# Two transformer layers on one core: a first pass fed from on-chip transposes, and a last layernorm's output written by Pool

## Chip, cores and metric

One NeuronCore of one Trainium2 chip. The metric is the device time of one launch in microseconds. Engines: PE (TensorE), DVE (VectorE), ACT (ScalarE), POOL (GpSimd, below also Pool) and SP (SyncE, which here only issues transfers).

## The reference, cut to what matters

x has 4 batches of 1024 tokens with 128 channels, 16 heads of 8 channels. Four residual blocks follow each other, each ended by a layernorm:

```python
x = _layernorm(x + L0_attn(x))   # q, k scaled to norm 1 per token; softmax over all 1024 keys; projection
x = _layernorm(x + L0_ffn(x))    # int8 quantised matmul 128x128
x = _layernorm(x + L1_attn(x))   # layernorm of q, k per head, rotary table, causal softmax; projection
x = _layernorm(x + L1_ffn(x))    # silu(gate) * up, hidden 384, then down
```

In layer 0's attention q and k are divided by their norm over the 128 channels of a token, and the scores by 8**0.5 and by the head's temperature.

## The kernel before

**Work.** The tokens are eight chunks of 512. Attention runs in 64 passes: a layer, a batch, a half of its queries (512) and a group of four heads. Passes are taken in pairs, and a pair is cut into steps; there are 400 steps. A step is two exps on ACT (`probs<-ps`, line 717, 128x1024 each) with the scores before them (`scores`, line 874, into one of three slots of two PSUM banks) and the sums behind them (`sums`, line 896, four heads side by side into the bank `ACC`). In layer 1 the steps on the causal diagonal are masked by Pool (`mask`, line 627) between the exp and the sums.

**Heads stacked by products.** A head's 8 channels of q and k are written as a high and a low part (tf32-like `fp32r`), and the four products of the parts are stacked as rows: in `q_st` and `k_st` each group of 32 rows (a head) holds 8 channels times 4 products. The stacks of a pass come from `parts_scratch` in DRAM: `send_parts` (line 449) writes the parts, `load_rows` (line 465) reads the rows. Pass 0 and pass 1 are special: their rows are copied from the tile `prep_part` by small transfers (`first_rows`, line 424, 64 KB each).

**Side work.** All that isn't attention is cut into units: projections, norms, transposes, the two feed-forward blocks. PE's units go through one PSUM bank (`SIDE`); DVE reads it and frees it (`side_filled`, `side_read`). Each lane of units (`p` for layer 0's q, k, v; `m` for the middle; `l` for the last block; `t` for what ends a pair) is in a fixed order. The table `ORDER` has one word for each of the 400 slots and one behind: it says how many units of which lane are run there, and with `<` or `|` whether the sums come behind the side units or between the two scores. PE, DVE, Pool and SP all build their programs from this table.

**The head**, before the first exp: DVE's `memset` feeds warm-up matmuls (`keep_warm`, line 930), PE makes q, k and v of chunks 0 and 1 in eight banks (line 938), ACT squares q and k of each token tile with a running sum (line 689), DVE takes the reciprocal root of 8 sums in nine small steps (`rows_norm`, lines 1103 and 259 to 271) and scales k and q (line 1117). PE transposes them (line 752), ACT and DVE cut them into parts (lines 700 and 1332 to 1336), and SP and ACT copy the rows of pass 0 with four transfers each. PE waits for `parts_ready` and `rows_in[0]`. The second half of the keys of pass 0 comes by four more transfers from SP (line 515), that of pass 1 through DRAM. `WARM` counts warm-up matmuls.

**Lines that the change touches besides:** the output of the last layernorm of chunks 0 to 6 (units `ln_out_y`, lane `l`; chunk 6 in lane `m`) is four `tensor_scalar` of 128x128 by DVE (line 1075, `yo<-last_y`), and SP stores `yo`. Chunk 7 is done by `end()`. The matmul of layer 0's feed-forward (`ffn`, line 838) is four bf16 matmuls of 128x128 for a chunk; other PE units are cut by `quarters` (line 763) into 32 output columns of the array at a time. Pool's program is a list sorted by slot:

```python
todo = [(s + 1, 0, "mask", s) for s in range(NS) if STEPS[s][3]]
...
todo += [(FIRST[p - 1], 3, "bias", p) for p in range(GB - 1, NP, GB)]
todo.sort(key=lambda x: x[:2])
```

Of the kernel before, what the change touches and what calls it, by code (L numbers as in the profile page):

```python
# [166 lines left out]
lp m m |t <mm mmp <mm <m p m <p <mpp <m <mp <m m <mtt <mm |m |tm
m p <m mp ll <mll m - ll < <l < |tl l l l - |l < l
- l < l < <llll l l |t | |tt mm m <t m mm <mm | |tmm |
|ttl l <lm <m |mm <mml mml m < m m mmm - l t mlm lm ml m |l  # L170
ml ml < <m l l l <ll <l <lm tt < tm <m <m |mm |m |mm |m mm
- |mmlmm | |tmm | |m m < m < m <l <m m m <m |tm | |tmtlm -
<m <ll mm ml < m < ll - <l | <l tl - | |l l l - <l
- <l < <l < <l <ll <l |lltt | |tm mm < t m < <mmm m |ttm |m
<tl <mmm - |mmm |ml |lm lm lm m m ml tlm |l ml lm l l l <mmlm l
# [1229 lines left out]
```

## Time and profile before

| | |
|---|---|
| median of 3 runs | 811.27 us (811.23 to 811.58) |
| the profiled execution | 810.68 us, span 808.6 us |
| PE busy | 791.6 us (98%) |
| ACT busy | 767.8 us (95%), of it 745.9 the 800 exps |
| DVE busy | 527.7 us (65%) |
| POOL busy | 174.7 us (22%) |
| granted TensorE clock | 0.998 |

The span runs from the first to the last instruction; 2.08 us of the profiled execution's time lie around it. A busy time is the union of an engine's instructions. PE's matmuls overlap each other, so that 98% doesn't say it is at its limit everywhere.

### The profile page before, as it was taken

Reading aid. Unit: us, or ns where it says so; the run is one execution under the profiler, and the core shown is the slowest. Engines: PE = TensorE matmul, PEld = TensorE weight load, DVE = VectorE, ACT = ScalarE, POOL = GpSimd, SP = SyncE. Lnnn points to the kernel's source line nnn. Section 1 sums busy time; section 2 is a strip of 40 time slices with the busy share of each in tenths; the row PEclk is TensorE's granted clock in tenths of the full one; section 3 lists DMA queues with packets and bytes.
Section 4 is the critical chain, followed back from the end, with each engine's and each line's share of the span. In section 5 each row is a group of like instructions: output and inputs, shape, how many; then the busy total and the mean of one; then the engine's idle time right before and its main releaser. Section 6 shows DMA issues by size and latency. Waiting matters only on the chain.

```text
span 808.6 us, 18428 instructions
## 1 busy us (share of the span) xinstructions
PE 791.6 (98%) x7469; PEld 295.9 (37%) x7469; DVE 527.7 (65%) x1422; ACT 767.8 (95%) x869; POOL 174.7 (22%) x370
## 2 busy tenths in 40 slices
PE   8999999999999999999999999999999999999996
PEld 4333333333333433443333433343333343443444
DVE  4253657758758788687862685766573387787646
ACT  4999999999999999999999999999999999999982
POOL 3111101101102601033100511023300263363220
PEclk9999999999999999999999999999999999999999
DMA  5776232415404711532170431231231231053000
GB/s 148 253 235 208 89 122 82 154 41 183 144 28 157 272 41 40 183 144 93 41 260 27 124 112 42 92 128 44 92 131 51 69 130 54 28 182 120 15 15 16
DMA packets 48553, 88.71 MB, mean 110 GB/s; under 512 B 5200, under 2 KB 14544, under 8 KB 48464
## 3 DMA queue, kind: packets, MB, share of 16 engines
q1 hardware_dynamic: 47696, 85.95, 31.2%
q8 instruction: 61, 1.00, 0.5%
q0 software_dynamic: 288, 1.05, 0.4%
q10 hardware_dynamic: 480, 0.48, 0.2%
q14 instruction: 28, 0.23, 0.1%
HBM read 50.50 MB, written 35.65 MB: 107 GB/s over the span
## 4 chain that ended last, share of the span: by engine, by line
PE 74%; ACT 14%; DVE 7%; issue 3%; POOL 1%; DMA 0%; ACTq 0%; DVEq 0%; POOLq 0%
PE ps L896 36%; PE ps L874 21%; ACT probs L717 13%; PE ps L763 8%; PE ps L752 3%; PE ps L849 2%; DVE th L1282 1%; DVE hT L1283 1%; PE ps L930 1%; PE ps L757 1%; ACT th L677 0%; PE ps L938 0%; DVE gate_sb L1279 0%; POOL v_all L590 0%; PE ps L791 0%
## 5 line engine op out<-in xcount | busy, mean ns | idle before, releaser
L717 ACT ACTIVATE probs<-ps 128x1024 f32<-128x1024 f32 x800 | 745.9, 1057 | 15.3 <-PE ps L874 11.3
L896 PE MATMUL ps<-probs,v_st 128*32 128x512 f32 (+3 forms) x3584 | 425.0, 556 | 3.3 <-issue 1.8
L874 PE MATMUL ps<-q_st,k_st 32*128 32x512 f32 (+3 forms) x1792 | 257.4, 459 | 2.1 <-ACT probs L717 0.9
L874 PEld LDWEIGHTS ps<-q_st,k_st 32*128 32x128 f32 x1792 | 119.6, 182 | 281.8 <-ACT probs L717 226.5
L627 POOL TENSOR_SCALAR_AFFINE_SELECT probs<-probs 128x256 f32<-128x256 f32 x256 | 104.3, 430 | 141.0 <-ACT probs L717 138.9
L896 PEld LDWEIGHTS ps<-probs,v_st 128*32 128x32 f32 x3584 | 79.9, 108 | 110.2 <-issue 80.9
L595 POOL COPY v_st<-v_all 128x256 f32<-128x256 f32 (+1 forms) x65 | 25.6, 402 | 343.3 <-PE ps L896 335.2
L1256 DVE COPY mid_qkv<-ps 128x384 f32<-128x384 f32 x32 | 17.8, 558 | 45.5 <-PE ps L763 43.8
L1137 DVE STREAM_TRANSPOSE sums_t<-ps 128x512 f32<-128x512 f32 x32 | 22.9, 717 | 29.1 <-PE ps L896 29.0
L1287 DVE TENSOR_TENSOR last_y<-ps,last_y 128x128 f32<-128x128 f32 x24 | 7.0, 292 | 42.6 <-PE ps L763 42.6
L849 PE MATMUL ps<-yTp,w_hid 128*128 128x512 f32 x84 | 30.8, 448 | 1.7 <-DVE gate_sb L1279 0.3
L1256 DVE COPY prep_qkv<-ps 128x384 f32<-128x384 f32 x24 | 13.4, 557 | 27.4 <-PE ps L763 27.0
L590 POOL COPY v_all<-mid_qkv 128x512 f32<-128x512 f32 x9 | 14.0, 1552 | 66.4 <-DVE mid_qkv L1256 61.5
L763 PE MATMUL ps<-w_cols,yT 128*32 128x384 f32 x256 | 26.8, 491 | 0.0
L763 PE MATMUL ps<-w_down,hT 128*32 128x128 f32 x672 | 23.9, 275 | 0.6 <-DVE last_y L1287 0.3
L1233 DVE TENSOR_TENSOR x_all<-ps,x_all 128x512 f32<-128x512 f32 x15 | 10.4, 692 | 20.5 <-PE ps L763 19.3
L1282 DVE SCALAR_TENSOR_TENSOR th<-th,gate_sb 128x512 f32<-128x512 f32 x21 | 14.7, 698 | 13.5 <-PE ps L849 10.8
L1279 DVE COPY gate_sb<-ps 128x512 f32<-128x512 f32 x21 | 14.5, 691 | 13.1 <-PE ps L849 12.8
L763 PEld LDWEIGHTS ps<-w_down,hT 128*32 128x32 f32 x672 | 17.9, 110 | 12.2 <-issue 6.8
L849 PEld LDWEIGHTS ps<-yTp,w_hid 128*128 128x128 f32 x84 | 12.5, 188 | 24.8 <-DVE gate_sb L1279 10.3
L617 POOL TENSOR_TENSOR x_all<-x_all,vecs 128x512 f32<-128x512 f32 x16 | 20.4, 1278 | 0.6 <-DMA x_all<-in_x 0.6
L763 PE MATMUL ps<-w_cols,xT 128*32 128x384 f32 x192 | 20.2, 492 | 0.0
(192 smaller groups left out, 636.2 us busy)
## 6 DMA issues: line engine op xcount, KB each, us to landing
k_st<-parts_scratch SPq DMA_DIRECT2D x46, 512.0 KB, 3.5
parts_scratch<-mid_part SPq DMA_DIRECT2D x34, 512.0 KB, 4.0
q_st<-parts_scratch SPq DMA_DIRECT2D x62, 256.0 KB, 3.9
parts_scratch<-prep_part SPq DMA_DIRECT2D x28, 512.0 KB, 4.3
k_st<-parts_scratch SPq DMA_DIRECT2D x17, 256.0 KB, 2.8
xT<-in_xT SPq DMA_DIRECT2D x8, 256.0 KB, 4.2
x_all<-in_x SPq DMA_DIRECT2D x8, 256.0 KB, 6.6
out<-yo SPq DMA_DIRECT2D x7, 256.0 KB, 2.3
```

Of the source, the lines that this page charges most:

```text
L595: return g_.tensor_copy(v_st[:, p % VB, t, :, p % 2 * SR:p % 2 * SR + D], v_all[:, layer, b % 2, t, g * GH * D:(g + 1) * GH * D] .rearrang ...
L617: g_.tensor_tensor(x_all[:, c, :, :], x_all[:, c, :, :], bc(vecs[:, 3 * layer, :].unsqueeze(1), [P, TC, C]), ALU.add).then_inc(bias_added, 1)
L627: op = g_.affine_select(out=block_, in_=block_, compare_op=ALU.is_ge, fill=0.0, base=0, pattern=[[0, 2], [1, P]], channel_multiplier=-1)
L717: nc.scalar.activation(probs[:, k % PS, :, 0:w], slot(k)[:, :, 0:w], ACT.Exp).then_inc(probs_ready, 1)
L752: last_ = tp(dst[:, t * P:(t + 1) * P], src(t), idn[:])
L763: last_ = mm(dst[row, :], src[:, row], w, start=first, stop=last)
L849: last_ = mm(side, w_hid[:, 0 if what == "gate" else 1, k * P:(k + 1) * P], yTp[:, n, :], start=(n == 0), stop=(n == PARTS - 1))
L874: last_ = mm(slot(k)[:, e, at:at + n], k_st[row, p % KB, kt * P:(kt + 1) * P], q_st[row, p % KB, lo:HALF], start=True, stop=not shifted)
L896: last_ = mm(acc[HR * h:HR * (h + 1), lo:HALF], v_st[:, p % VB, kt, h, :], probs[:, (2 * s + h // 2) % PS, h % 2, at:at + n], start=FIRST[ ...
L1137: v.transpose(sums_t[:], acc).then_inc(sums_turned, 1)
L1256: v.tensor_copy(job[name]["qkv"][:, k, :], side[:, 0:3 * C]).then_inc(side_read, 1)
L1282: chain[lane(name, c)].link(stt(out=th[:, k % 2, :], in0=th[:, k % 2, :], scalar=1.0, in1=gate_sb[:, k % 2, :], op0=ALU.add, op1=ALU.mult))
```

## The change

Five edits.

1. **The head of pass 0.** Q, k and v of chunk 0 are made by twelve 128x128 matmuls into three banks (q, k, v). ACT squares only q; k's sums of squares come from DVE's `bn_stats` and `bn_aggr`. DVE scales only the 32 channels of the pass's four heads, each written four times side by side (`first_qk`), so that PE's transposes give the stack's rows at once. ACT multiplies them by a sign column, rounding to the high part, and DVE adds or leaves the low part and writes `k_st` and `q_st`. No transfer lies on this way.
2. **What follows the head.** The full q and k of chunk 0 are scaled, transposed and cut after the first scores have been issued, the rows of pass 1 go out in small transfers from SP and Pool, and the second half of pass 0's keys comes from a unit `firstT` on PE and DVE. Pass 1's second half comes by four direct transfers.
3. **The output of layer 1's last layernorm** of chunks 0 to 6 goes to Pool (`norm_out`).
4. **ffn** is cut into `quarters`.
5. **`ORDER`** is another table; late weights are fetched after x's first chunk has come.

```diff
-       [(e, n + "_y" if n == "ln_out" else n, 1) for e, n, k in LN_UNITS]
+       [("pool", "ln_out_y", 1) if n == "ln_out" else (e, n, 1) for e, n, k in LN_UNITS]
...
-FIRST_KEYS = [("prep", 1, "pe", "qkT", 1), ("prep", 1, "dve", "scale_q", 0), ("prep", 1, "pe", "qkT", 0)]
+FIRST_KEYS = [("prep", 1, "pe", "firstT", 1), ("prep", 1, "dve", "scale_k", 0), ("prep", 1, "pe", "qkT", 1), ("prep", 1, "dve", "scale_q", 0), ("prep", 1, "pe", "qkT", 0)]
...
-p p p - - - - <pc < <p - p < <cpp <pp - <t c <p <pp
+- - | <p pp p <p < p < p < <p <p p p |pt <p < <pp
...
-    WARM = (10, 4, 0, 22, 7)
+    HEAD_SQUARES = 2
+    WARM = (8, 3, 8, (4, 5, 7))
...
         load_x(1)
+        sp.wait_ge(x_in[0], 16)
...
         for u, dst in ((1, k_st), (0, q_st)):
-            sp.wait_ge(parts_ready, 2 - u)
-            for y in range(PRODUCTS // 2):
-                first_rows(sp, 0, u, dst, y)
-        for u, dst in ((1, k_st), (0, q_st)):
-            for y in range(PRODUCTS):
-                first_rows(sp, 1, u, dst, y)
+            for low in range(PARTS - u):
+                sp.wait_ge(*((parts_ready, 2 - u) if low else (head_high, 2 - u)))
+                for y in range(PRODUCTS):
+                    if (y % PARTS if u else y // PARTS) == low and (u, y) != (0, PRODUCTS - 1):
+                        first_rows(sp, 1, u, dst, y)
...
+        def norm_out(c):
+            tok_ = tok[lane("last", c)]
+            s_, y2 = tok_["st"], tok_["y2"]
+            if c:
+                pool.wait_ge(y_out, c * 16)
+            pool.wait_ge(out_root, c + 1)
+            for t in range(TC):
+                op = g_.tensor_scalar(yo[:, t, :], y2[:, t, :], s_[:, 0, 2 * t:2 * t + 1], s_[:, 2, t:t + 1], ALU.subtract, ALU.mult)
+            op.then_inc(out_ready, 1)
...
+        todo += [(slot_of("last", c, "ln_out_y", 1), 4, "norm_out", c) for c in range(NCH - 1)]
...
+            act.wait_ge(head_qkv, 1)
             for t in range(TC):
+                square(t, ps[:, ACC, t * P:(t + 1) * P], job["prep"]["st"][:, 0, 2 * t:2 * t + 1])
...
+                if t == HEAD_SQUARES:
                     act.wait_ge(tcol_made, 1)
+                    for u in (1, 0):
+                        act.wait_ge(first_turned, 2 - u)
+                        nc.scalar.activation(first_sign[:, u, :], ps[:, FIRST_BANK[u], :], ACT.Copy,
+                                             scale=(sign_q, sign_k)[u]).then_inc(first_signed, 1)
...
-                    last_ = mm(side[:, t * P:(t + 1) * P], xqT[:, t * P:(t + 1) * P], w_ffn[:], start=True, stop=True)
+                    last_ = quarters(side[:, t * P:(t + 1) * P], xqT[:, t * P:(t + 1) * P], w_ffn[:])
...
-                    pe.wait_ge(rows_in[p % KB], 32 * (p // KB + 1) + (32 * PRODUCTS - 32 if p % KB < 2 else 0))
+                    pe.wait_ge(*((first_made, 2) if not p else (rows_in[p % KB], 32 * (p // KB + 1) + {0: -32, 1: 32 * PRODUCTS - 80}.get(p % KB, 0))))
+                    if p == 1:
+                        pe.wait_ge(low_rows_in, 16 * (PARTS + 1))
...
+            if not s:
+                pe.wait_ge(parts_ready, 2)
...
-                elif what == "ln_out_y":
-                    if c:
-                        dve.wait_ge(y_out, c * 16)
-                    layernorm(ln, what, y2, yo, out_ready)
                 elif what in ("ln_stats", "ln_aggr", "ln_rs1", "ln_rs2"):
-                    layernorm(ln, what, y2 if k else x_all[:, c], None)
+                    if (ln, what, k) == ("last", "ln_aggr", 0) and c:
+                        dve.wait_ge(out_ready, c)
+                    layernorm(ln, what, y2 if k else x_all[:, c], None, out_root if (name, what, k) == ("last", "ln_rs2", 1) else None)
...
+            for t in range(TC):
+                ch.step(v.bn_stats(bn[:, t, :], by_t(side)[:, t, :]))
+            ch.need()
+            for t in range(TC):
+                ch.step(v.bn_aggr(mv[:, 2 * t:2 * t + 2], bn[:, t, :]))
+            ch.need()
+            ch.link(stt(out=mean2, in0=mean, scalar=float(C), in1=mean, op0=ALU.mult, op1=ALU.mult))
+            ch.link(stt(out=per(0, 0)[:, :, 1], in0=var, scalar=float(C), in1=mean2, op0=ALU.mult, op1=ALU.add))
+            dve.wait_ge(norms_ready, TC)
+            roots(0)
+            for u in (1, 0):
+                op = tt(first_qk[:, :, u, :, :], by_t(ps[:, ACC + u, :])[:, :, 0:HR].unsqueeze(3).to_broadcast([P, TC, HR, PRODUCTS]),
+                        per(0, 1)[:, :, u].unsqueeze(2).unsqueeze(3).to_broadcast([P, TC, HR, PRODUCTS]), ALU.mult)
+                op.then_inc(first_scaled, 1)
+            flags(1)
+            for u, dst in ((1, k_st[:, 0, 0:HALF]), (0, q_st[:, 0, :])):
+                dve.wait_ge(first_signed, 2 - u)
+                stt(out=dst, in0=ps[:, FIRST_BANK[u], :], scalar=(low_q, low_k)[u], in1=first_sign[:, u, :].bitcast(F32),
+                    op0=ALU.mult, op1=ALU.add).then_inc(first_made, 1)
```

PE's queue up to the first scores, before (`L930` is a warm-up matmul, `L938` q, k, v, `L752` transposes, `L874` scores):

```order
L930 MATMUL ps<-warm 128x512 x10
L938 MATMUL ps<-w_cols,xT 128x384 x8
L930 MATMUL ps<-warm 128x512 x4
L752 MATMUL ps<-ident,prep_qk 128x128 x8
L930 MATMUL ps<-warm 128x512 x22
L951 TENSOR_LOAD far_any
L951 ISA x2
L982 COMPARE_AND_BRANCH
L874 MATMUL ps<-q_st,k_st 128x512 x6
```

and now, to the first sums (`L962` warm-up, `L970` and `L975` q, k, v of chunks 0 and 1, `L982` and `L778` transposes, `L904` scores, `L928` sums):

```order
L962 MATMUL ps<-warm 128x512 x8
L970 MATMUL ps<-w_cols,xT 128x128 x12
L975 MATMUL ps<-w_cols,xT 128x384 x4
L962 MATMUL ps<-warm 128x512 x3
L982 MATMUL ps<-ident,prep_qkv 128x128 x8
L962 MATMUL ps<-warm 128x512 x8
L987 TENSOR_LOAD far_any
L987 ISA x2
L1026 COMPARE_AND_BRANCH
L904 MATMUL ps<-q_st,k_st 128x512 x6
L778 MATMUL ps<-ident,prep_qk 128x128 x8
L904 MATMUL ps<-q_st,k_st 128x512 x4
```

The transposes behind the first scores are those that stood ahead of them; the ones ahead are of the repeated channels.

DVE's queue in the head as it is now, from the scaling of the repeated channels (`L1391`) to the parts of the full q (`L1409`); `L1397` writes the stacks of pass 0, `L1400` scales the full q and k:

```order
L1391 TENSOR_TENSOR prep_qkv<-ps,prep_st 128x4x128 x2
L1063 TENSOR_SCALAR far<-cst 128x1
L1064 TENSOR_REDUCE cst<-small 128x2
L1065 SCALAR_TENSOR_TENSOR cst<-cst 128x2
L1066 SCALAR_TENSOR_TENSOR cst<-cst 128x1
L1067 TENSOR_SCALAR far<-cst 128x1
L1068 TENSOR_TENSOR far_any<-far 128x1
L1397 SCALAR_TENSOR_TENSOR k_st<-ps,w_cols,mid_part 128x512
L1397 SCALAR_TENSOR_TENSOR q_st<-ps,w_cols,mid_part 128x512
L1400 TENSOR_TENSOR prep_qk<-ps,prep_st 128x4x128 x2
```

The stacks are written ahead of the full q and k, and six small steps on the flags lie between.

Pool's queue around the output of chunk 4 as it is now (`L636` is the layernorm's output, `L646` the masks, `L603` copies of v, `L625` a bias):

```order
L603 COPY v_st<-v_all 128x32x8
L625 TENSOR_TENSOR x_all<-x_all,vecs 128x512
L636 TENSOR_SCALAR yo<-last_y,last_tok 128x128 x4
L646 AFFINE_SELECT probs<-probs 128x2x128 x6
L603 COPY v_st<-v_all 128x32x8
```

Six masks stand behind the output and its wait for DVE's root.

## Rows read from the trace of the kernel before

**Rows 1.** The page, busy time of each engine.

```profile
PE 791.6 (98%) x7469; PEld 295.9 (37%) x7469; DVE 527.7 (65%) x1422; ACT 767.8 (95%) x869; POOL 174.7 (22%) x370
```

**Rows 2.** Waits of ACT: line, releaser, us in total, times, longest.

```profile
ACT probs L717 <- PE ps L874: 11.3, 28, 4.1
```

**Rows 3.** Timeline of ACT: start, length, what, [idle before and releaser]; first and last exps.

```profile
19.83 126.84 ACT L717 ACTIVATE probs<-ps 128x1024 f32<-128x1024 f32 x137 [4.08 <-PE ps L874]
...
782.88 2.86 ACT L717 ACTIVATE probs<-ps 128x1024 f32<-128x1024 f32 x3 [0.20 <-PE ps L874]
```

**Rows 4.** Groups by form: busy us, mean ns | idle before.

```profile
L717 ACT ACTIVATE probs<-ps 128x1024 f32<-128x1024 f32 x800 | 745.9, 1057 | 15.3 <-PE ps L874 11.3
```

**Rows 5.** Stretch 700 to 780: columns us, PE, PEld, DVE, ACT, POOL busy.

```profile
700.00:780.00 80.00, 78.00 (x987) 35.08 (x980) 53.84 (x143) 75.82 (x84) 33.70 (x75) 1.00 0.24 81
```

**Rows 6.** Timeline of the head, all engines.

```profile
1.27 4.45 PE L930 MATMUL ps<-warm 128*128 128x512 bf16 x10 [1.27 <-DVE warm L997]
...
5.51 5.63 PE L938 MATMUL ps<-w_cols,xT 128*128 128x384 f32 x16
...
6.66 0.28 ACT L689 ACTIVATE attn<-ps 128x128 f32<-128x128 f32 x1 [3.63 <-PE ps L938]
...
9.91 0.59 ACT L695 ACTIVATE v_all<-ps 128x512 f32<-128x512 f32 x1
10.04 0.17 DVE L1103 TENSOR_SCALAR prep_st<-prep_st 128x8 f32<-128x8 f32 x1 [1.55 <-ACT attn L689]
...
11.87 1.29 DVE L1117 TENSOR_TENSOR prep_qk<-ps,prep_st 128x512 f32<-128x512 f32 x2
...
12.61 1.32 PE L752 MATMUL ps<-ident,prep_qk 128*128 128x128 f32 x8
...
14.03 0.69 ACT L700 ACTIVATE prep_part<-ps,w_cols 128x512 fp32r<-128x512 f32 x1 [0.42 <-PE ps L752]
...
14.88 0.75 DVE L1336 SCALAR_TENSOR_TENSOR prep_part<-ps,w_cols,prep_part 128x512 fp32r<-128x512 f32 x1 [0.16 <-DVE prep_part L1333]
...
15.27 0.48 ACT L703 ACTIVATE mid_qkv<-ps 128x384 f32<-128x384 f32 x1
...
19.27 0.33 PEld L874 LDWEIGHTS ps<-q_st,k_st 32*128 32x128 f32 x6 [1.09 <-issue]
19.30 0.73 PE L874 MATMUL ps<-q_st,k_st 32*128 32x512 f32 x6 [0.63 <-DMA q_st<-prep_part]
```

**Rows 7.** The chain that ended last, head: start, us, what.

```profile
16.97 2.20 DMA q_st<-prep_part
```

**Rows 8.** Timeline of the tail: like operations on 128x128 tiles.

```profile
789.74 0.97 DVE L1190 BATCH_NORM_STATS2 last_bn<-ps 128x6 f32<-128x128 f32 x4 [0.32 <-PE ps L783]
...
790.75 0.38 DVE L1065 BATCH_NORM_AGGREGATE last_tok<-last_bn 128x2 f32<-128x6 f32 x4
...
801.27 0.97 PEld L811 LDWEIGHTS ps<-w_down,hT 128*128 128x128 f32 x8
```

**Rows 9.** Groups by form: the output on DVE, Pool's nearest work, ffn.

```profile
L617 POOL TENSOR_TENSOR x_all<-x_all,vecs 128x512 f32<-128x512 f32 x16 | 20.4, 1278 | 0.6 <-DMA x_all<-in_x 0.6
...
L1075 DVE TENSOR_SCALAR yo<-last_y,last_tok 128x128 f32<-128x128 f32 x24 | 8.6, 422 | 0.1
...
L838 PE MATMUL ps<-w_ffn,xqT 128*128 128x128 bf16 x32 | 3.2, 222 | 0.2
```

**Rows 10.** Timeline of DVE and Pool around the output of chunk 4.

```profile
721.30 0.16 DVE L271 SCALAR_TENSOR_TENSOR last_tok<-last_tok 128x4 f32<-128x4 f32 x1
...
722.46 1.32 DVE L1075 TENSOR_SCALAR yo<-last_y,last_tok 128x128 f32<-128x128 f32 x1
...
722.43 1.27 POOL L617 TENSOR_TENSOR x_all<-x_all,vecs 128x512 f32<-128x512 f32 x1
723.65 2.20 POOL L627 TENSOR_SCALAR_AFFINE_SELECT probs<-probs 128x256 f32<-128x256 f32 x6
```

**Rows 11.** Timeline of ACT at the same place.

```profile
720.26 14.77 ACT L717 ACTIVATE probs<-ps 128x1024 f32<-128x1024 f32 x16 [0.23 <-PE ps L874]
```

More of the change, by code:

```diff
@@ L167 @@
[L167 to L175, printed above, removed]
@@ L666, in _ @@
                 mask(n)
+            elif what == "send":
+                send_parts(pool, "prep", n, 1)
             elif what == "load":
                 load_v(n)
+            elif what == "norm_out":
+                norm_out(n)
             else:
@@ L696, in head @@
             for t in range(TC):
-                if t == TC - 1:
+                act.wait_ge(head_qkv, 4 + t)
+                for u in range(2 if t < HEAD_SQUARES else 0):
+                    square(TC + 2 * t + u, ps[:, t, u * C:(u + 1) * C], job["mid"]["st"][:, 0, 2 * t + u:2 * t + u + 1])
+                if t == HEAD_SQUARES:
                     act.wait_ge(tcol_made, 1)
-                    act.wait_ge(head_turned, 2)
-                    nc.scalar.activation(job["prep"]["part"][:, 0, 0, :], head_bank[0], ACT.Copy, scale=tcol).then_inc(head_high, 1)
@@ L710, in _ @@
+                nc.scalar.activation(job["mid"]["qkv"][:, t, :], ps[:, t, 0:3 * C], ACT.Copy).then_inc(
+                    qkv_copied if t == TC - 1 else head_copied, 1)
         head()
@@ L846, in stage @@
                 last_ = turn4(lambda t: buffers(name, c)["qk"][:, t, k * C:(k + 1) * C], side, ident)
+            elif what == "firstT":
+                pe.wait_ge(first_scaled, 3)
+                last_ = turn4(lambda t: first_qk[:, t, k, :, :].rearrange("p f y -> p (f y)"), side, ident)
             elif what in ("gate", "up"):
@@ L974, in steps @@
                 for name, c, e, what, k in SIDE_ORDER[s]:
-                    if e == "pe" and (name, c, e, what, k) != FIRST_KEYS[0] and \
-                            not (shifted and (name, c, e, what, k) in FIRST_KEYS):
+                    if e == "pe" and not (shifted and (name, c, e, what, k) in FIRST_KEYS):
                         stage(name, c, what, k)
@@ L1258, in read @@
                     got()
+            elif what == "firstT":
+                chain[name].link(ts(first_sign[:, k, :], side, sign_k, None, ALU.mult))
+                stt(out=k_st[:, 0, HALF:S], in0=side, scalar=low_k, in1=first_sign[:, k, :].bitcast(F32),
+                    op0=ALU.mult, op1=ALU.add).then_inc(side_read, 1)
             elif what == "qkT":
@@ L1339, in _ @@
+        first_consts()
+        flags(0)
+        head()
         units(FIRST_KEYS)
```

262 lines of the change are left out of this document (153 added, 109 removed).

## Prediction

> **What bounds the kernel now.** I read the page first. PE is busy for 98% and ACT for 95% of the span, DVE for 65%, POOL for 22% [rows 1]: two engines are candidates. The waits of ACT decide between them. Its exps waited for PE's scores for 11.3 us in 28 places, and 4.1 us of that is the wait before the first exp [rows 2]; in the rest of the kernel 7.2 us are left. The timeline gives the frame: the first exp starts at 19.83 us, the last group of three starts at 782.88 and ends at 785.74 [rows 3]. Between these lie 765.9 us, and the 800 exps alone are busy for 745.9 of them [rows 4]. So the span is a head of 19.83, a stretch bound by ACT, and a tail of 808.6 - 785.74 = 22.9. PE isn't far behind: from 700 to 780 it is busy for 78.0 of 80 us and ACT for only 75.8 [rows 5], so late in the kernel PE sets the pace here and there. DVE and POOL have room in every stretch, so work taken from DVE alone shortens nothing unless PE waits for DVE.
>
> The change can therefore act in three places: the head (19.83), the 7.2 us of waits behind it, and the tail.
>
> **The head.** Before, the first exp waits for PE, PE for the last transfer of q's rows (2.20 us from 16.97, [rows 7]; scores start at 19.30, [rows 6]). Now that transfer isn't on the way. I follow the new chain with the old durations.
>
> - PE starts q, k, v where the old matmuls start, 5.51; two warm-up matmuls of 4.45 / 10 = 0.44 less make no difference, since w_cols is what is waited for [rows 6]. I take 5.2 to 5.5. The 128x128 fp32 matmuls need 0.97 / 4 = 0.24 us each, four of them being eight records in the tail [rows 8]. Q is done at about 6.3, k at 7.3, v at 8.3, the four wide ones of chunk 1 (5.63 / 8 = 0.70 each) at 11.1.
> - ACT squares q from 6.5: a square with its read takes (9.91 - 6.66) / 8 = 0.41 [rows 6], so q's four are done at 8.2. DVE meets k at 7.5: 0.97 for four `bn_stats`, 0.4 for four `bn_aggr` [rows 8], two small steps of 0.2: 9.3. ACT is not late.
> - The root took from 10.04 to 11.87, 1.83 us [rows 6]: done at 11.1. Before, it started at 10.04, so 0.7 us is won: k's norm no longer waits for eight squares in a row.
> - Scaling, two of 0.645 (1.29 for both): 12.4. Transposes, 0.66 each and behind the scaling: 13.2. ACT's sign and rounding, 0.69 each [rows 6]: k at 13.3, q at 14.0. DVE's six steps on the flags (1.2) end at 13.6 and hide under ACT. The stacks, 0.75 each: 14.4 and 15.1.
> - PE also waits for ACT's last two copies of chunk 1 (`qkv_copied`), 0.48 each behind the sign: 15.0. Then comes the branch. Its price isn't shown alone: PE's weight load stood idle for 1.09 us over warm-up, flag, branch and rows [rows 6], so it lies between 0 and 1.1. I take 0.3, because that gap ends 0.1 us after the transfer has landed and so is mostly the transfer's.
>
> Scores at 15.4 and the first exp 0.53 later (19.83 - 19.30), at 15.9. **Gain: 3.9 us**, with 2.8 to 4.4 as bounds.
>
> **What follows the head** can take some of it back. The rows of pass 1 are needed at exp 8, ideally at 15.9 + 8 x 0.93 = 23.4, so its scores at 22.9 (0.93 is 126.84 / 137, [rows 3]). DVE scales the full k and q behind the stacks: 15.1 to 16.4. PE transposes behind three scores: k at 17.3, q at 18.0. DVE's four parts of 0.69 to 0.75 end at 20.4. SP's last of four transfers of q and k is issued at about 20.9 and lands 2.2 us later: 23.1 to 23.5. Pool's last one is about as late. So exp 8 is late by 0.3 to 0.7. Then `firstT` and both full transposes (0.66 each) come on PE within four slots, with a spare of some 0.4 us in a slot: DVE's second root for chunk 1 ends near 24.4, `firstT` is asked for near 24.3, and the second transpose can cost another 0.3. The rows of pass 2 come about when they do now but are needed 3.9 us earlier; before, 137 exps ran without a wait [rows 3], so there is slack, of a size that no row here gives. I charge **0.8 us**, bounds 0 and 2.
>
> **Pool's output.** 28 `tensor_scalar` leave DVE, 24 of them with a mean of 0.422 us and 8.6 us busy, 1.4 for a chunk [rows 9], and come to Pool. Pool's price for one isn't shown. From below it is nothing, from above the 1278 ns of its 128x512 sum [rows 9]; a quarter of that, 0.32, has the same columns, and I take it: 1.3 us a chunk, 9 us for all. Pool has 80 - 33.7 us free from 700 to 780 [rows 5]. DVE's time isn't what ends a wait, except where PE waits for DVE to free the side bank; a block of 1.4 us less on DVE in seven places may take 0.2 us out of ACT's waits. The tail stays: chunk 7 is done by the same code.
> Here the trace shows contention: DVE's output at 722.46 took 1.32 us against a mean of 0.42 [rows 9], just as long as Pool's sum over 722.43 to 723.70 lasted [rows 10]. The Trainium skill has the rule (SBUF — State Buffer, section "SBUF: two separate sides"): DVE's two-port operations and GpSimd share one port pair under an exclusive lock, and the loser waits for the whole instruction. The trace agrees. By that rule Pool's 28 operations hold DVE up in turn, up to 0.32 us each, 9 us over the kernel; DVE has over a third of its time free [rows 1], so in the sum it is nothing, and it is a part of the third rival. The skill also calls an elementwise operation on GpSimd about half as fast as on VectorE (GPSIMD Engine Reference, section "3.1 Elementwise — side-by-side cycle accounting"), which would make the block 2 x 1.4 = 2.8 us; no row here shows this operation on Pool, and the sum stays.
>
> **Ffn in quarters:** 32 matmuls in 3.2 us before, 0.4 a chunk [rows 9]. Now 128. From below nothing changes, from above four times as much, +1.2 a chunk; PE has slack around most of them. I take 0.1 in all.
> **The table:** both have 400 slots and nearly the same units in every 20 of them. It can win at most the 7.2 us of waits, and I have no row that says it wins; I take 0.2, bounds -2 and +2.
>
> **Sum:** -3.9 + 0.8 - 0.2 + 0.1 - 0.2 = -3.4 us. The profiled execution took 810.68 (span 808.6), 0.6 under the median of 811.27. Against itself it gives 807.3, in the runs' terms 811.27 - 3.4 = **807.9 us**. A measurement of this kernel tells about 0.2% from no change, 1.6 us, so the bound of "faster" is 809.65.
>
> **Rivals.**
> 1. *The head's gain is given back at once.* The branch costs its 1.1, and pass 1's rows, `firstT` or pass 2's rows cost 2: -3.1 + 2 = -1.1, 810.2. For it: DVE and PE run one behind the other through all of it. Against it: warm-ups fill the slack, and ACT can be caught up only while PE has a reserve of slots.
> 2. *The table and the lighter DVE also end the late waits.* Half of the 7.2 us beyond the forecast would be 3; I take 2: 805.9. For it: PE is full from 700 to 780. Against: nothing is taken from PE, and that is where the waits end.
> 3. *Pool's masks queue behind the output* (ends slower). `norm_out` waits for DVE's root, and masks stand behind it. In slot 366 the root of chunk 4 ended at 721.46 [rows 10]. From 720.26 on [rows 11] to the last one [rows 3] the timeline has 63 exps, so step 366 ended at 717.2: DVE was 4.2 us behind ACT. Pool waits for the root of slot 368, then takes 1.3 for the output, 0.4 to 0.8 for masks (2.20 / 6 = 0.37 each, [rows 10]), and PE wants the masks about 1.5 steps (2.8 us) after the exps. That makes a stall of 0 to 3 us, in those places where masks follow at once: chunks 1 and 4, less so 5. It decides from about 2 us on in both, and to be slower than before it needs 3 us in both: -3.4 + 6 = +2.6, 813.9. Against it: chunk 1 has two slots between root and output, and DVE has one block less.
> 4. The change doesn't do what it says: pass 0 would still wait for something that lands at 19. No transfer feeds `k_st` and `q_st` there, so I give this no more than the rest.
>
> **Chances.** Forecast 0.62, rival 1 0.16, rival 2 0.12, rival 3 0.07, the rest 0.03. Range 805.7 to 810.4: it takes in rival 2 and rival 1 and leaves rival 3 out. Faster: forecast 0.60, rival 2 0.12, a part of rival 1 0.07, together 0.79. Same 0.13. Slower 0.08.
>
> **What would show it.** The first exp at 15.9 (15.4 to 17.0). No transfer among the releasers of the first scores. A wait of at most 0.7 at exp 8. PE's waits behind the head near 7 us in all. `yo` on Pool with some 0.3 us each and no stall of the sums behind the masks of steps 230 and 369. The last exp ends 22.9 us before the end. A first exp later than 17.5, or ACT's waits behind the head over 10 us, makes the prediction wrong.

## The result, and the profile after

| | before | after |
|---|---|---|
| time of the runs, median (us) | 811.25 (810.69 to 811.58, 4) | 821.89 (821.05 to 823.59, 4) |
| profiled execution, its span (us) | 810.68, 808.6 | 821.05, 819.0 |
| mean granted clock of TensorE | 0.998 | 0.991 |

The ratio is 1.0136, 95% interval 1.0122 to 1.0151: slower by 10.6 us, where 3.4 us faster was forecast.

The page of the changed kernel and the waits of ACT, beside [rows 1] and [rows 2]:

```profile
PE 792.2 (97%) x7572; PEld 297.5 (36%) x7574; DVE 536.6 (66%) x1415; ACT 767.1 (94%) x854; POOL 197.3 (24%) x401
...
L743 ACT ACTIVATE probs<-ps 128x1024 f32<-128x1024 f32 x800 | 746.9, 1053 | 25.2 <-PE ps L904 20.5
...
L636 POOL TENSOR_SCALAR yo<-last_y,last_tok 128x128 f32<-128x128 f32 x24 | 19.3, 815 | 16.6 <-DVE last_tok L271 16.6
```

```profile
ACT probs L743 <- PE ps L904: 20.5, 36, 5.1
```

Pool has 22.6 us more to do, and each of its output operations takes 815 ns in the mean where DVE's took 422 [rows 9]. (The median is 796 against 346 ns; DVE's mean has operations in it that were held up, as in [rows 10].) ACT's waits for scores grew from 11.3 to 20.5 us although the first of them shrank. The timeline of ACT (start, length, what, [idle before and its releaser]) shows where; its first and last rows answer to [rows 3]:

```profile
15.08 7.44 ACT L743 ACTIVATE probs<-ps 128x1024 f32<-128x1024 f32 x8 [0.76 <-PE ps L904]
23.42 115.74 ACT L743 ACTIVATE probs<-ps 128x1024 f32<-128x1024 f32 x125 [0.90 <-PE ps L904]
...
458.40 5.61 ACT L743 ACTIVATE probs<-ps 128x1024 f32<-128x1024 f32 x6 [0.95 <-PE ps L904]
469.14 1.94 ACT L743 ACTIVATE probs<-ps 128x1024 f32<-128x1024 f32 x2 [5.14 <-PE ps L904]
471.73 2.85 ACT L743 ACTIVATE probs<-ps 128x1024 f32<-128x1024 f32 x3 [0.65 <-PE ps L904]
474.97 35.82 ACT L743 ACTIVATE probs<-ps 128x1024 f32<-128x1024 f32 x38 [0.38 <-PE ps L904]
```

```profile
651.17 1.94 ACT L743 ACTIVATE probs<-ps 128x1024 f32<-128x1024 f32 x2 [1.88 <-PE ps L904]
653.66 1.03 ACT L743 ACTIVATE probs<-ps 128x1024 f32<-128x1024 f32 x1 [0.55 <-PE ps L904]
655.09 39.79 ACT L743 ACTIVATE probs<-ps 128x1024 f32<-128x1024 f32 x42 [0.41 <-PE ps L904]
...
736.79 1.94 ACT L743 ACTIVATE probs<-ps 128x1024 f32<-128x1024 f32 x2 [2.16 <-PE ps L904]
739.14 5.74 ACT L743 ACTIVATE probs<-ps 128x1024 f32<-128x1024 f32 x6 [0.41 <-PE ps L904]
745.19 1.02 ACT L743 ACTIVATE probs<-ps 128x1024 f32<-128x1024 f32 x1 [0.31 <-PE ps L904]
...
794.43 1.02 ACT L743 ACTIVATE probs<-ps 128x1024 f32<-128x1024 f32 x1 [0.16 <-PE ps L904]
```

The first exp starts at 15.08 in place of 19.83: 4.75 us won, and no transfer releases its scores (DVE's writing of `q_st` does). The tail is 819.0 - 795.45 = 23.6 us, 0.7 more. Between them lie 780.4 us in place of 765.9, so 14.5 us were lost there. Three places hold 12.8 of them: 0.95 + 5.14 + 0.65 + 0.38 = 7.1 us behind the output of chunk 1, 2.8 behind that of chunk 3 and 2.9 behind that of chunk 4. Exp 8 comes 0.90 late.

**Chunk 1.** Pool, PE and DVE in the timeline of that place:

```profile
452.15 3.13 POOL L636 TENSOR_SCALAR yo<-last_y,last_tok 128x128 f32<-128x128 f32 x4
...
455.24 3.64 POOL L646 TENSOR_SCALAR_AFFINE_SELECT probs<-probs 128x256 f32<-128x256 f32 x10
...
456.74 0.38 DVE L1112 BATCH_NORM_AGGREGATE mid_tok<-mid_bn 128x2 f32<-128x6 f32 x4
...
456.86 1.07 PE L928 MATMUL ps<-probs,v_st 128*32 128x256 f32 x16 [1.38 <-POOL probs L646]
457.15 7.64 DVE L1115 TENSOR_SCALAR mid_tok<-mid_tok 128x4 f32<-128x4 f32 x1
...
458.83 0.39 POOL L603 COPY v_st<-v_all 128x256 f32<-128x256 f32 x1
459.19 1.27 POOL L625 TENSOR_TENSOR x_all<-x_all,vecs 128x512 f32<-128x512 f32 x1
...
460.43 2.20 POOL L646 TENSOR_SCALAR_AFFINE_SELECT probs<-probs 128x256 f32<-128x256 f32 x6
...
462.58 0.39 POOL L603 COPY v_st<-v_all 128x256 f32<-128x256 f32 x1
462.93 1.84 POOL L646 TENSOR_SCALAR_AFFINE_SELECT probs<-probs 128x256 f32<-128x256 f32 x5
464.83 0.17 DVE L259 TENSOR_SCALAR mid_tok<-mid_tok 128x4 int32<-128x4 int32 x1
...
465.62 0.72 DVE L1184 STREAM_TRANSPOSE sums_t<-ps 128x512 f32<-128x512 f32 x1
...
466.44 1.93 PE L928 MATMUL ps<-probs,v_st 128*32 128x512 f32 x8 [4.64 <-issue]
```

Two things are to be seen. The ten masks at 455.24 stand behind the output's 3.13 us, and PE's sums wait 1.38 us for them: that is the third rival. The second is new: an operation of DVE on 128x4 numbers, the addition of the epsilon in the middle layernorm of chunk 5, lasts 7.64 us. Its like lasts 0.17. It ends at 464.79, and Pool's queue went idle at 464.77. Behind it on DVE stands the turn of the sums (465.62: DVE transposes the bank `ACC`, and PE's next sums need that bank). PE stood still for it for 4.64 us, and then goes on at half the clock: the granted clock from 468 to 470 is 0.50, and a group of eight sums takes 1.93 us in place of 1.06.

```profile
468.00:470.00 2.00, 2.00 (x18) 0.90 (x18) 1.93 (x6) 0.86 (x1) 0.00 (x0) 0.50 0.00 0
```

**Chunks 4 and 3.** In chunk 4 a like operation of DVE is held too, for 4.17 us:

```profile
733.88 0.38 DVE L1112 BATCH_NORM_AGGREGATE last_tok<-last_bn 128x2 f32<-128x6 f32 x4 [0.96 <-POOL yo L636]
734.30 4.17 DVE L1115 TENSOR_SCALAR last_tok<-last_tok 128x4 f32<-128x4 f32 x1
...
734.65 1.38 PE L928 MATMUL ps<-probs,v_st 128*32 128x512 f32 x8 [2.21 <-POOL probs L646]
```

But PE was waiting for something else there: its sums at 734.65 stood still for 2.21 us for Pool's masks, and nothing that PE waited for stood behind the held operation. In chunk 3 no DVE operation is held at all, and the sums wait for masks in the same way:

```profile
649.17 1.23 PE L928 MATMUL ps<-probs,v_st 128*32 128x512 f32 x8 [1.96 <-POOL probs L646]
```

After both waits the clock is at 0.50 for some 3 us (650 to 653, 736 to 738), which belongs to the price of the late masks.

The stretch of [rows 5] (length; busy time and count of PE, PEld, DVE, ACT, POOL; granted clock; DMA share; GB/s), where PE was busy for 78.00 and Pool for 33.70 us:

```profile
700.00:780.00 80.00, 75.90 (x902) 33.07 (x896) 56.50 (x139) 73.71 (x81) 38.59 (x82) 0.98 0.27 87
```

### The profile page after: what moved, and what is told of

Its sections match the earlier page's. It is cut to its first block, busy times and chain, and to the rows that moved or that the text cites. A ratio compares the mean times of both kernels' runs of the same rounds, so it can differ in the third digit from the quotient of the medians.

```text
span 819.0 us, 18627 instructions
## 1 busy us (share of the span) xinstructions
PE 792.2 (97%) x7572; PEld 297.5 (36%) x7574; DVE 536.6 (66%) x1415; ACT 767.1 (94%) x854; POOL 197.3 (24%) x401
## 3 DMA queue, kind: packets, MB, share of 16 engines
q0 software_dynamic: 384, 1.25, 0.5%
## 4 chain that ended last, share of the span: by engine, by line
PE 72%; ACT 11%; DVE 8%; issue 4%; POOL 3%; DMA 1%; SPq 0%; ACTq 0%; DVEq 0%; POOLq 0%
PE ps L928 36%; PE ps L904 20%; ACT probs L743 10%; PE ps L789 8%; PE ps L778 4%; PE ps L877 2%; POOL probs L646 1%; POOL yo L636 1%; DVE th L1332 1%; DVE hT L1333 1%; PE ps L783 1%; DMA xT<-in_xT 0%; ACT th L705 0%; DMA q_st<-prep_part 0%; DVE gate_sb L1329 0%
## 5 line engine op out<-in xcount | busy, mean ns | idle before, releaser
L743 ACT ACTIVATE probs<-ps 128x1024 f32<-128x1024 f32 x800 | 746.9, 1053 | 25.2 <-PE ps L904 20.5
L928 PE MATMUL ps<-probs,v_st 128*32 128x512 f32 (+3 forms) x3584 | 429.3, 562 | 12.2 <-POOL probs L646 5.8
L904 PE MATMUL ps<-q_st,k_st 32*128 32x512 f32 (+3 forms) x1792 | 257.3, 461 | 2.0 <-ACT probs L743 1.5
L904 PEld LDWEIGHTS ps<-q_st,k_st 32*128 32x128 f32 x1792 | 119.6, 183 | 280.2 <-ACT probs L743 222.0
L646 POOL TENSOR_SCALAR_AFFINE_SELECT probs<-probs 128x256 f32<-128x256 f32 x256 | 103.5, 428 | 119.0 <-ACT probs L743 115.6
L928 PEld LDWEIGHTS ps<-probs,v_st 128*32 128x32 f32 x3584 | 80.5, 109 | 122.0 <-issue 95.6
L603 POOL COPY v_st<-v_all 128x256 f32<-128x256 f32 (+1 forms) x65 | 24.3, 376 | 329.5 <-PE ps L928 327.2
L1329 DVE COPY gate_sb<-ps 128x512 f32<-128x512 f32 x21 | 14.5, 692 | 14.9 <-PE ps L877 14.4
L1332 DVE SCALAR_TENSOR_TENSOR th<-th,gate_sb 128x512 f32<-128x512 f32 x21 | 15.9, 757 | 12.1 <-PE ps L877 10.9
L636 POOL TENSOR_SCALAR yo<-last_y,last_tok 128x128 f32<-128x128 f32 x24 | 19.3, 815 | 16.6 <-DVE last_tok L271 16.6
L625 POOL TENSOR_TENSOR x_all<-x_all,vecs 128x512 f32<-128x512 f32 x16 | 20.6, 1289 | 3.6 <-DMA x_all<-in_x 3.6
```

The source lines that it names most:

```text
L603: return g_.tensor_copy(v_st[:, p % VB, t, :, p % 2 * SR:p % 2 * SR + D], v_all[:, layer, b % 2, t, g * GH * D:(g + 1) * GH * D] .rearrang ...
L636: op = g_.tensor_scalar(yo[:, t, :], y2[:, t, :], s_[:, 0, 2 * t:2 * t + 1], s_[:, 2, t:t + 1], ALU.subtract, ALU.mult)
L646: op = g_.affine_select(out=block_, in_=block_, compare_op=ALU.is_ge, fill=0.0, base=0, pattern=[[0, 2], [1, P]], channel_multiplier=-1)
L743: nc.scalar.activation(probs[:, k % PS, :, 0:w], slot(k)[:, :, 0:w], ACT.Exp).then_inc(probs_ready, 1)
L904: last_ = mm(slot(k)[:, e, at:at + n], k_st[row, p % KB, kt * P:(kt + 1) * P], q_st[row, p % KB, lo:HALF], start=True, stop=not shifted)
L928: last_ = mm(acc[HR * h:HR * (h + 1), lo:HALF], v_st[:, p % VB, kt, h, :], probs[:, (2 * s + h // 2) % PS, h % 2, at:at + n], start=FIRST[ ...
```

## The experiments

Times are medians; the ratio is to runs of the kernel before on the same chip, with its 95% interval. All but the fourth start from the changed kernel.

| kernel | us | ratio |
|---|---|---|
| outputs of all seven chunks on DVE (`all_dve`) | 809.59 | 0.9988 (0.9979 to 0.9997) |
| chunks 1, 3, 4 on DVE, the others on Pool (`split_134`) | 809.14 | 0.9981 (0.9972 to 0.9990) |
| chunk 1 alone on Pool (`pool_1`) | 816.57 | 1.0074 (1.0059 to 1.0090) |
| kernel before, outputs on Pool (`old_pool`) | 823.72 | 1.0160 (1.0145 to 1.0176) |
| `all_dve`, old table from slot 7 on (`all_dve_table`) | 811.22 | 1.0005 (0.9996 to 1.0014) |
| `all_dve`, ffn not in quarters (`all_dve_ffn`) | 809.45 | 0.9988 (0.9979 to 0.9997) |
| `all_dve`, four spare operations on Pool (`spare_1`) | 811.66 | 1.0014 (1.0004 to 1.0023) |
| outputs of chunks 1 and 3 later, 4 on DVE (`late_out`) | 808.30 | 0.9971 (0.9960 to 0.9982) |
| the change, turn moved forward (`turn_first`) | 821.82 | 1.0145 (1.0128 to 1.0162) |
| `pool_1`, turn moved forward (`pool_1_turn`) | 816.81 | 1.0074 (1.0057 to 1.0091) |
| `pool_1`, DVE with four operations more (`pool_1_pad`) | 819.71 | 1.0105 (1.0088 to 1.0122) |
| `pool_1`, waits between the four operations (`pool_1_gaps`) | 811.69 | 1.0012 (1.0002 to 1.0022) |
| the change, the same waits (`after_gaps`) | 818.01 | 1.0086 (1.0072 to 1.0100) |
| `pool_1`, one wait behind the four (`pool_1_end`) | 811.39 | 1.0007 (0.9997 to 1.0016) |

### Which edit costs, and which chunk

`ON_DVE` names the chunks whose output DVE makes, as before; it is (1, 3, 4) in the second kernel and (0, 2, 3, 4, 5, 6) in `pool_1`.

```diff
+ON_DVE = (0, 1, 2, 3, 4, 5, 6)
-                if e != "pool":
+                if e != "pool" or c in ON_DVE:
-        todo += [(slot_of("last", c, "ln_out_y", 1), 4, "norm_out", c) for c in range(NCH - 1)]
+        todo += [(slot_of("last", c, "ln_out_y", 1), 4, "norm_out", c) for c in range(NCH - 1) if c not in ON_DVE]
```

> The changed kernel with edit 3 undone: the last layernorm's outputs of chunks 0 to 6 are DVE's again, the head, ffn and table stay. Theory (Pool's outputs cause the loss): the trace of the change has waits of 7.1 us at chunk 1, 2.8 at chunk 3 and 2.9 at chunk 4 (12.8 in all), all behind an output on Pool; without them 821.9 falls by 11 to 14 us, to 808 to 811, and with the head's 3.9 us gain it should lie under the kernel before: 806 to 809. Rival (the new table or the clock loses): the waits near 458, 469, 651 and 737 stay, and it stays over 815.

> As the change, but only chunks 0, 2, 5 and 6 are output by Pool; 1, 3 and 4, where masks follow at once, by DVE. Theory (Pool's output costs only where masks queue behind it): within 1 us of all_dve, 806 to 809. Rival (Pool's outputs cost everywhere, by 3.1 us each or by holding DVE up): 2 us or more above all_dve.

> As all_dve, with chunk 1's output alone on Pool. Theory: the two waits near 458 and 469 come back, 6 to 7.5 us above all_dve, with a stretch of half clock of 3 to 7 us. Rival (the loss is a sum of all seven outputs' backlog): 1 to 3 us above all_dve.

> The kernel before with edit 3 alone: outputs of chunks 0 to 6 on Pool, old head, old table. Theory (the loss is Pool's output and not the new table): slower than before by 8 to 20 us; here the roots of chunks 3, 4 and 6 stand in the very slot of the output, so Pool waits for them longer. Rival (it is the new table together with it): within 3 us of 811.3.

With every output on DVE the kernel takes 809.59 us, 0.12% under the kernel before; so edit 3 costs 1.48% (1.0136 - 0.9988), 12.0 us, and the other four together win 1.0 (0.2 to 1.7 by the interval). In the profile ACT's waits are 8.9 us, with none over 0.9 behind the head. Chunks 0, 2, 5 and 6 can have their output on Pool for nothing (809.14). Chunk 1 alone on Pool costs 0.86%, 7.0 us, and repeats the rows of the change (0.95, 5.11, 0.65, 0.40 us; a DVE operation of 7.60 us). That leaves 5 us for chunks 3 and 4, if the places add up; neither was run alone. The fourth kernel has only edit 3: 13.0 us slower than before. With the old table the places differ (ACT waits 2.17 us at chunk 1, 1.43 at chunk 3, 6.79 at chunk 4), and the sum is much the same. No DVE operation of over 1.5 us stands in any of these places; the 6.79 us are masks that queue behind an output which itself waits for DVE's root, and PE's sums behind the wait of 6.06 us take 1.93 us in place of 1.07:

```profile
725.79 3.13 POOL L632 TENSOR_SCALAR yo<-last_y,last_tok 128x128 f32<-128x128 f32 x4 [4.90 <-DVE last_tok L271]
...
728.87 3.29 POOL L642 TENSOR_SCALAR_AFFINE_SELECT probs<-probs 128x256 f32<-128x256 f32 x9
...
730.51 1.93 PE L914 MATMUL ps<-probs,v_st 128*32 128x256 f32 x16 [6.06 <-POOL probs L642]
```

Neither the head nor the new table makes edit 3 dear.

### The small edits

```diff
-                    last_ = quarters(side[:, t * P:(t + 1) * P], xqT[:, t * P:(t + 1) * P], w_ffn[:])
+                    last_ = mm(side[:, t * P:(t + 1) * P], xqT[:, t * P:(t + 1) * P], w_ffn[:], start=True, stop=True)
```

> all_dve (809.6) with the slot table of the kernel before from slot 7 on (slots 0 to 6 must fit the new head). If the new table takes back a part of the head's gain when DVE does the outputs (all_dve's waits of ACT behind the head are 8.2 us against 7.2 before, and its tail is 1.0 us longer), this is 1 to 2.5 us under all_dve, 807 to 808.5. If the new table is better in itself, it is over 810.

> all_dve with ffn as four bf16 matmuls of 128x128 again. If quarters cost PE time that ACT feels: 0.5 to 2 us under all_dve. If they are free: within 0.5 us of it.

The old table was the worse one with the new head, by 1.6 us (1.4 by the ratios), which I hadn't expected: its profile has waits of 1.25 us at exp 8, of 0.41 at 34.55 and of 1.73 at 40.05, the last two of which the new table doesn't have. The quarters cost nothing (809.45 and 809.59).

### Late masks alone: four spare operations on Pool

```diff
+        todo += [(slot_of("last", 1, "ln_out_y", 1), 4, "spare", 1)]
...
+            elif what == "spare":
+                for t in range(TC):
+                    if t:
+                        pool.wait_ge(spare_done, t)
+                    g_.tensor_scalar(spare[:], ident[:], ident[:, 0:1], ident[:, 1:2], ALU.subtract, ALU.mult).then_inc(spare_done, 1)
```

> all_dve, and Pool does four tensor_scalar of 128x128 on a spare tile where the change has the output of chunk 1 (slot 230); it waits for no root, and DVE does all seven outputs. Theory (Pool's 3.1 us ahead of the masks are the cost): the waits near 458 and 469 come back and it is 5 to 7.5 us above all_dve, like pool_1. Rival (the wait for the root or the store's semaphore is the cost): within 1 us of all_dve.

A miss: 2.1 us over `all_dve`, not 5 or more. The masks were as late as in the change (3.49 us of spare work ahead of them), and ACT waited 1.24 + 0.40 us, but no DVE operation ahead of the turn was held and the clock stayed up. That suggests that late masks cost 2 us, and that the other 5 of chunk 1 come from DVE. The kernel differed from `pool_1` in two ways, though: DVE reached the place 1.5 us later, and Pool's four operations waited one for the other. Both are taken apart below.

### The turn ahead of the held operation

In `ORDER`, slots 230 to 233:

```diff
-|tl m <mm tmm
+|tl - < tmmmmm
```

> The change with Pool's outputs as they are, and DVE's table changed in slots 231 to 233 alone: the turn of the sums now stands ahead of the middle layernorm of chunk 5, so that the small DVE operation that was held for 7.64 us in the changed kernel comes behind the turn and not ahead of it. Theory (of the 7 us of ScalarE's waits around 458 to 475 us, about 2 are masks that come late and about 5 are the turn that queues behind the held operation, with the half clock that follows): the 5.14-us wait goes, the matmul group at 466 us is back near 1.1 us, the waits there add up to 1 to 3 us, and the time is 815 to 818 us. Rival (the late masks alone): the order on DVE does not matter, and the time stays at 820 us or more.

> The same move of the turn in the kernel that makes chunk 1's output alone on Pool (816.6 us with the turn behind). Theory: the 5.11-us wait goes and with it 3 to 5 us, so 811.5 to 813.5 us, near the kernel with four spare operations at the same place (811.7). Rival (the late masks alone): 816 to 817 us as before. If the turn itself is held by Pool's queue in the same way as the small operation, both kernels change by less than 1 us.

Both are misses. The time stayed, as the rival said, but not by its reason. Timeline of the change with the turn moved:

```profile
460.93 0.72 DVE L1184 STREAM_TRANSPOSE sums_t<-ps 128x512 f32<-128x512 f32 x1 [5.41 <-PE ps L928]
...
462.06 2.69 DVE L1188 TENSOR_TENSOR heads_t<-sums_t,rd 128x256 f32<-128x256 f32 x1
...
466.64 1.06 PE L928 MATMUL ps<-probs,v_st 128*32 128x512 f32 x8
...
472.84 0.58 PE L778 MATMUL ps<-ident_b,xq 128*128 128x128 bf16 x4 [3.27 <-DVE xq L1223]
...
474.19 1.02 ACT L743 ACTIVATE probs<-ps 128x1024 f32<-128x1024 f32 x1 [3.13 <-PE ps L904]
```

The turn is in time (460.93 in place of 465.62), the 5.14-us wait is gone and the sums at 466.64 run at full clock. But DVE stood idle for 5.41 us ahead of the turn, and the operation behind it was held for 2.69 us. The layernorm of chunk 5 comes after that: its `xq` is ready at 472.69, where `all_dve` has it at 468.28. PE waits 3.27 us for it, and ACT 3.13 and 1.56 us behind that. My expectation left out that chunk 5's layernorm is as urgent as the turn; the move of the turn put the wait elsewhere and ended none.

### What holds DVE

In this order: DVE with more work, waits between Pool's four operations, one wait behind them.

```diff
+                elif what == "ln_out_y" and c == 1:
+                    for t in range(TC):
+                        ch.link(ts(spare[:], y2[:, t, :], s_[:, 0, 2 * t:2 * t + 1], s_[:, 2, t:t + 1], ALU.subtract, ALU.mult))
...
+                if t:
+                    pool.wait_ge(out_step, t)
                 op = g_.tensor_scalar(yo[:, t, :], y2[:, t, :], s_[:, 0, 2 * t:2 * t + 1], s_[:, 2, t:t + 1], ALU.subtract, ALU.mult)
-            op.then_inc(out_ready, 1)
+                op.then_inc(out_step if t < TC - 1 else out_ready, 1)
...
             op.then_inc(out_ready, 1)
+            pool.wait_ge(out_ready, c + 1)
```

> Chunk 1's output alone on Pool (816.6 us), and DVE besides computes the same four blocks into a spare tile, ahead of the middle layernorm of chunk 5, so that DVE has 1.4 to 1.8 us more to do and meets Pool's full queue that much later. Theory (5 of the 7 us are DVE, which is locked out from 457.6 us for 7.6 us; with four spare operations on Pool and DVE 1.5 us later it was not): the 7.6-us operation is back under 1 us, the turn is in time, ScalarE's waits near 458 to 475 us fall from 7.1 to 1.5 to 2.5 us and the time to 811 to 813 us, so more work makes the kernel faster. Rival (Pool's full queue locks DVE out whenever they meet, and the four spare operations were cheap for another reason): a DVE operation of 5 us or more remains, now a later one, and the time is 816 to 819 us.

> Chunk 1's output alone on Pool, and each of the four operations waits for the one before by a semaphore, as the four spare ones did; they take 3.4 to 3.6 us in place of 3.13, and the masks behind them stand just as late. If the gaps between Pool's operations were why the spare four cost 2 us and not 7, the time falls from 816.6 to 811 to 813 us. If it was DVE's 1.5 us, it stays at 816 to 817.5 us with a DVE operation held for 7 us or more.

> The change with one thing added: each of Pool's four output operations of a chunk waits by a semaphore for the one before, as in the kernel with chunk 1 alone, where that took the time from 816.6 to 811.7 us. Theory (DVE is held until Pool's queue runs dry where the four went out back to back, and gets its turn between Pool's instructions where they did not): no DVE operation of over 3 us at 457 and 734 us, ScalarE's waits behind the head down from 20 to 12 to 15 us, of them 1.5 to 2.5 us at each of chunks 1, 3 and 4 from masks that come late, and 813 to 816 us. If the gaps helped chunk 1 by chance, chunk 4 keeps its 4-us operation or chunk 1 its 7.6 us, and the time stays at 818 us or more.

> Chunk 1's output alone on Pool, its four operations back to back as in the change, and one wait behind the last of them, for its own semaphore, ahead of the first mask. It tells whether the run of four sets DVE's fate or only that the masks follow it without a gap. If one gap between output and masks is enough: DVE's small operation at 457 us under 0.5 us and 811 to 813 us. If the four back to back are what counts: the 7.6-us operation stays, and 816 to 817.5 us.

More work on DVE was no cure, and my guess about the 1.5 us fell: the four added operations lasted 10.18 us together (the first of them 9.04, the others 0.35 each), ACT's wait grew to 7.87 us and the time to 819.7. DVE's work at this place is the same as in `spare_1`, where the four lasted 1.61 us; what differs on Pool is the waits between its operations, and the tile that they read. The waits on Pool were a cure. With a wait between each two of the four the kernel takes 811.7 us, and with a single wait behind them 811.4, 5.2 us less than `pool_1` (5.4 by the ratios). The masks are no earlier for it. DVE and Pool in the timeline of the last one:

```profile
457.27 0.43 DVE L1117 TENSOR_SCALAR mid_tok<-mid_tok 128x4 f32<-128x4 f32 x1
457.74 0.32 DVE L260 TENSOR_SCALAR mid_tok<-mid_tok 128x4 int32<-128x4 int32 x1
...
461.46 0.72 DVE L1186 STREAM_TRANSPOSE sums_t<-ps 128x512 f32<-128x512 f32 x1 [2.32 <-PE ps L930]
...
462.60 2.69 DVE L1190 TENSOR_TENSOR heads_t<-sums_t,rd 128x256 f32<-128x256 f32 x1
```

```profile
452.26 3.14 POOL L637 TENSOR_SCALAR yo<-last_y,last_tok 128x128 f32<-128x128 f32 x4
455.48 3.65 POOL L648 TENSOR_SCALAR_AFFINE_SELECT probs<-probs 128x256 f32<-128x256 f32 x10
459.07 0.40 POOL L604 COPY v_st<-v_all 128x256 f32<-128x256 f32 x1
459.44 1.28 POOL L626 TENSOR_TENSOR x_all<-x_all,vecs 128x512 f32<-128x512 f32 x1
460.67 2.21 POOL L648 TENSOR_SCALAR_AFFINE_SELECT probs<-probs 128x256 f32<-128x256 f32 x6
```

Pool does the same as before (3.14 us, then ten masks, the copy, the sum and six masks without a gap), and the masks start 0.08 us after the output's end, where in the change they follow at once. But the operation that was held for 7.6 us now lasts 0.43 and the one behind it 0.32, about the length of one mask (0.365). So DVE got its turn between two instructions of Pool here, and didn't in `pool_1`. The added wait isn't the only way to that, and a full queue of Pool isn't enough to hold DVE: in `all_dve`, with no wait added, Pool ran from 456.80 to 463.64 without a gap, and DVE's small operations took 0.25 to 0.33 us beside its masks and its sum:

```profile
458.87 0.30 DVE L1116 TENSOR_SCALAR mid_tok<-mid_tok 128x4 f32<-128x4 f32 x1
```

```profile
459.11 2.20 POOL L647 TENSOR_SCALAR_AFFINE_SELECT probs<-probs 128x256 f32<-128x256 f32 x6
```

Nor is it cured for good in `pool_1_end`: at 462.60 an operation is held for 2.69 us, until Pool's queue is empty, with nothing urgent behind it.

In the whole change the waits between the four bring 3.9 us (818.0), less than the 6 to 9 I expected. No DVE operation of over 2 us is left; ACT's waits at the three places are 2.1, 1.7 and 4.3 us. Chunk 4's grew, although the operation that was held there is short now (0.23 us): the hold had cost nothing in that place. What is left, 7.9 us over `all_dve` by the ratios, is mostly the masks behind an output of 3.5 to 3.7 us and the lower clock that follows.

### A version that beats both

In `ORDER`, the unit of chunk 1's output goes from slot 230 to 239, that of chunk 3 from 328 to 338:

```diff
+ON_DVE = (4,)
...
-|tl m <mm tmm m - < |mm |tm |
+|t m <mm tmm m - < |mm |tm |l
...
-|tl | |tt < <mm <mtmm m m < <m |t <tm
+|t | |tt < <mm <mtmm m m < <m |tl <tm
```

> The change with the outputs of chunks 1 and 3 moved in the table from slots 230 and 328 to 239 and 338, behind the run of masked steps, still on Pool; chunk 4's on DVE, the rest on Pool. Theory (it matters where on Pool's queue the output stands, not how much Pool does): within 1 us of split_134 (809.1). Rival (Pool's 3.1 us cost wherever they are): 2 us or more above it.

It takes 808.30 us, 0.29% under the kernel before and 1.65% under the change. (From `split_134`, 809.14, it isn't apart: the intervals overlap.) Pool makes chunk 1's output at 466.75, in a gap of its own, and ACT has no wait between 447.00 and 500.31:

```profile
447.00 53.31 ACT L744 ACTIVATE probs<-ps 128x1024 f32<-128x1024 f32 x57
```

```profile
466.36 0.40 POOL L604 COPY v_st<-v_all 128x256 f32<-128x256 f32 x1
466.75 3.72 POOL L637 TENSOR_SCALAR yo<-last_y,last_tok 128x128 f32<-128x128 f32 x4
```

## Why the prediction was wrong

**The step that failed** is the term of edit 3, -0.2 us, which measured +12.0 us. Two sentences made it small.

The first is "Pool's price for one isn't shown ... a quarter of that, 0.32, has the same columns, and I take it". Measured: 0.815 us for one and 3.13 a chunk, where 1.3 was taken. The row it came from was the nearest engine row but not the nearest operation: a plain sum of two tiles says nothing of a `tensor_scalar` with two operands per partition. The sentence on the Trainium skill (GPSIMD Engine Reference, section "3.1 Elementwise — side-by-side cycle accounting": about half as fast as on VectorE, from a sum of two tiles) stood beside it with 2.8 us a chunk. The trace has a little more: by busy time 19.3 against 8.6 us for 24 operations, 2.2 times, and by the medians 796 / 346 = 2.3. Going by DVE's own row for this operation would have come nearer as well.

The second is on contention: I wrote that Pool's operations hold DVE up "up to 0.32 us each", and that "in the sum it is nothing" because DVE has a third of its time free. The trace before suggested it (one DVE operation as long as one sum on Pool, [rows 10]), and so does the Trainium skill (SBUF — State Buffer, section "SBUF: two separate sides": the loser waits for the whole instruction). In many places it went like that (0.32 us beside a mask, 1.20 beside a sum), but in chunk 1 the loser waited for some twenty instructions. `pool_1` against `pool_1` with one wait puts 5.2 us on it. Free time of an engine in the mean is no cover for an operation with the turn of the sums behind it.

**The third rival** (chance 0.07) had the mechanism for the larger part of the 12.0 us: masks queue behind the output, and PE's sums wait for them. With the holds gone 7.9 us are left (`after_gaps` against `all_dve`), a little more than the masks alone, since the waits lengthen each output by some 0.35 us. In chunk 1 late masks cost 1.8 to 2.1 us (`pool_1` with one wait, four spare operations; 1.5 to 2.1 by the ratios), where 3 were charged; the rest falls on chunks 3 and 4, and chunk 3 wasn't in the rival. With the old table ACT waited 6.8 us in chunk 4 alone. That PE goes on at the lower clock after such a wait wasn't in any case. **What no case had** is the hold of DVE, 5.2 of the 7.0 us of chunk 1.

**The head** was right in kind and in size: first exp at 15.9 forecast, 15.08 measured, and 14.68 to 16.09 in the profiles of all the kernels with the new head, so part of the 4.75 us is luck of one execution. (The 0.24 us for a 128x128 matmul was read off a row of weight loads [rows 8]; it came out right: twelve took 2.92 us.) **Behind it** 0.8 was charged; exp 8 waited for 0.78 to 1.29 us. **The gain that stays** is less than forecast even with the outputs on DVE: -1.0 and not -3.2 us. In the profile of `all_dve` against before the head gives -5.0, the tail takes 1.0 (0.3 to 0.4 of it goes when Pool makes chunk 6's output, as in `split_134` and `late_out`; 0.7 goes with the old table, `all_dve_table`) and the stretch between 2.0, of which waits are 1.0 and small gaps the rest. This sums to -2.0; its profiled execution, 808.46, was the fastest of 11, and the median is 1.1 above it. So the first rival, with 810.2 us, was nearer than the forecast for edits 1, 2, 4 and 5. **Ffn** costs nothing (0.1 forecast). **The table** brings 1.6 us with the new head (0.2 forecast): it ends waits at 34 and 40 us, and it lay inside the bounds of 2 either way.

The range was too narrow since the upper bound of Pool's price, 1.28 us, was named but never carried through: it makes 5.1 us a chunk, 3.8 more than the 1.3 taken. In the three places where masks follow at once that could be up to 11 us, an estimate that puts the slow case well above 815.

## What to carry to other kernels

Before work is moved to an engine that looks idle, list what stands behind it on that engine's queue and when it is due: the same four operations cost nothing in chunks 0, 2, 5 and 6, and 7 us in chunk 1 in front of masks. Price the operation by its own row on the old engine times a ratio, and carry the upper bound through to the time. If an operation on DVE or Pool is many times longer than its like, look at what the other of the two does to its very end. A single semaphore wait in the busy one's queue is a cheap thing to try; it won 5 us in the one place tried with it alone, and the condition isn't known.
